# Edge counting of a graph network: the one-hot operands of VectorE read from a table by register address, and the byte split and digit sums moved by some groups

## The chip, the cores and the metric

The kernel runs on one core of one Trainium2 chip. The metric is device time in microseconds (us): the median of the runs before is 2482.77 us, of three runs from 2481.85 to 2486.41. The profile shown here is one execution of 2481.51 us, in which 2480.0 us pass from the first to the last instruction.

## The reference, cut to what matters

3125 nodes of 128 features, 103125 edges (each of 50000 random pairs in both directions and a loop at each node), one type of four per edge. The edges are sorted by `dst`.

```
deg  = maximum(segment_sum(ones, dst), 1);  d = deg ** -0.5
h    = relu(layernorm(x))
feat = h
for i in range(10):                                   # ten hops
    agg  = segment_sum(feat[src] * (d[dst] * d[src])[:, None], dst)
    feat = (0.9 * agg + 0.1 * h) * r[i] + (1 - r[i]) * feat
x    = x + feat
emb  = relu(layernorm(x))
for _ in range(4):                                    # four gated steps
    m   = (emb @ W_msg.T + b_msg).reshape(n, 4, 128)
    emb = gru(segment_sum(m[src, type], dst), emb)
out  = x + emb
```

## The kernel before, in words

Both loops multiply by the adjacency matrix, so the kernel first **counts** the edges into a table `big1` in SBUF (counts per source tile, target tile and node, packed as small digits by type) and then does all gathers as matmuls against it. The change touches the counting alone.

**Counting.** The 103125 edges are 825 chunks of 125. The nodes are 125 groups (`Q`) of 25 targets. For each group q the sorted edges lie in a window of at most 8 chunks (`W`), which begins at chunk `lo`; `windows[q]` holds `lo` and `windows[q + MANY]` the number of chunks over 8, which is zero nearly always. Three tables lie in SBUF with a chunk to a column and an edge of it to a partition: `keys`, and `tab[:, 0]` (the source's place, 0 to 124) and `tab[:, 1]` (the weight). Group q takes these steps:

- GpSimd (POOL), `stage_window` (L384 to L397): waits until the buffer of four groups ago is used (`s_hot_used`), then copies the window of the tables into `win_place`, `win_f` (each entry doubled), `win_w` and `win_key` (doubled, less the group's offset): four small instructions, then `s_wst`.
- VectorE (DVE), `onehots(q, b)` (L1023 to L1057): loads `many` from `windows` into a register; waits for `s_wst` and `s_hot_used`; makes `marks` (8 chunks x 128 places, equal or not; L1038) and `hot_pair` (8 x 228 pairs; L1040); waits for its own `marks`; makes the last three chunks of `weighed` (`marks` times the weight; L1043); branches past the code for further chunks if `many` is zero (L1045). Each entry is doubled so that two neighbouring 16-bit elements are read as a pair.
- ScalarE (ACT), `weigh` (L513 to L517): five activations scale the first five chunks of `marks` into `weighed` by `win_w`.
- TensorE (PE), `count` (L658 to L681): eight matmuls of `weighed` by `hot_pair` add into one of the eight PSUM banks; then `s_hot_used`.
- ScalarE, `evacuate` (L491 to L498): two groups later the bank goes to `words`, a column of its block.

All one-hot buffers are four deep (`DEPTH`), so VectorE can be at most four groups ahead of TensorE.

**Blocks.** Eight groups (`BQ`) are a block; there are 16 (`NB`), the last of five groups. When a block's eight columns are in `words`, ScalarE splits its bytes into `packed` in three instructions, `part_lane` 0, 1, 2 (L500 to L511), of 1800, 1800 and 1400 bytes a partition. They stand in its order at groups 3, 4 and 5 of the next block. Lane 0 waits until `packed` of two blocks ago has been summed and stored. Then VectorE, `sum_digits(blk, b)` (L1059 to L1070), makes the digits in five instructions (L1064 to L1068) and writes them into `big1`. In VectorE's order these stand after group 6 of the next block; the first of them waits for the bytes (`s_bytes`). The SyncE queue stores each `packed` to HBM.

**Order.** Each engine's order is written out by hand. VectorE's counting is eight groups in a row, then a loop of three rounds of four blocks (`Fori`, register-held q), then two blocks in line, the last five groups, `sum_digits(14)`, the mean and variance of `x` (L1125 to L917), and `sum_digits(15)`. Then TensorE sums the degrees from `big1` (L712), and the hops and steps follow.

Of the kernel before, what the change touches and what calls it, by code (L numbers as in the profile page):

```python
# [7 lines left out]
ALU = mybir.AluOpType  # L8
ACT = mybir.ActivationFunctionType
AX = mybir.AxisListType  # L10
ds = bass.ds
# [5 lines left out]
Q = N // TILES  # L17
# [70 lines left out]
def build(nc, x, src, dst, edge_type, layer_reg, w_msg, b_msg, w_ih, w_hh, b_ih, b_hh, out):  # L88
# [7 lines left out]
    with ctx:  # L96
        def sb(name, shape, dt, where=None):
            return (where or ctx).enter_context(nc.sbuf_tensor(name, shape, dt))

        def sem(name):  # L100
            return ctx.enter_context(nc.semaphore(name))
# [63 lines left out]
        with ExitStack() as b:  # L165
            keys = sb("keys", [128, PAD], F32, b)
            tab = sb("tab", [128, 2, PAD], F16, b)
            win = sb("win", [128, 2, 2, W], F32, b)
            win_key = sb("win_key", [128, DEPTH, W, 2], F16, b)
            win_place = sb("win_place", [128, DEPTH, W, 2], F16, b)  # L170
            win_f = sb("win_f", [128, DEPTH, W, 2], F16, b)
            win_w = sb("win_w", [128, DEPTH, W], F32, b)
            win_p = sb("win_p", [128, 2, W], F16, b)
            win_x = sb("win_x", [128, 3], F32, b)
            hot_pair_x = sb("hot_pair_x", [128, KP], F16, b)
            hot_place = sb("hot_place", [128, 2, 128, W], F16, b)
            hot_place_x = sb("hot_place_x", [128, 128], F16, b)
            iota_pair = sb("iota_pair", [128, KP], F16, b)
            iota_row = sb("iota_row", [128, 128], F16, b)
            iota_place = sb("iota_place", [128, 128, W], F16, b)  # L180
            q_off = sb("q_off", [128, QB], F32, b)
            stat_x = sb("stat_x", [128, TILES, 6], F32, b)
# [84 lines left out]
        s_sq, s_sqr = sem("variance_made"), sem("root_made")  # L267
        s_prep = sem("staging_free")
        s_wst, s_pairs, s_hot_used = sem("window_staged"), sem("pair_onehots_made"), sem("onehots_used")
        s_marks, s_weighed = sem("place_onehots_made"), sem("place_onehots_weighed")  # L270
        s_weighed_d = sem("last_places_weighed")
        s_xs_g = sem("extra_weighed")
# [79 lines left out]
        def _(pool):  # L352
# [32 lines left out]
            def stage_window(q, b):  # L385
                lo = pool.value_load(windows[0:1, ds(q, 1)], min_val=0, max_val=NCH)
                pool.wait_ge(s_hot_used, q + 1)

                def twice(m):
                    return m.rearrange("p (w o) -> p w o", o=1).broadcast_to([CH, W, 2])  # L390

                pool.tensor_copy(win_place[0:CH, b, :, :], twice(tab[0:CH, 0, ds(lo, W)]))
                pool.tensor_copy(win_f[0:CH, b, :, :], twice(tab[0:CH, 1, ds(lo, W)]))
                pool.tensor_copy(win_w[0:CH, b, :], tab[0:CH, 1, ds(lo, W)])  # L394
                pool.tensor_tensor(win_key[0:CH, b, :, :], twice(keys[0:CH, ds(lo, W)]),  # L395
                                   q_off[0:CH, ds(q, 1)].rearrange("p (w o) -> p w o", o=1).broadcast_to([CH, W, 2]),
                                   ALU.subtract).then_inc(s_wst, 1)  # L397
# [50 lines left out]
        def _(act):  # L448
# [21 lines left out]
            act.wait_ge(s_prep, 1)  # L470
            act.wait_ge(s_wout, 1)

            act.wait_ge(s_const, 10)
            act.wait_ge(s_win_in, 16)
            act.sem_inc(s_taken, BANKS)
# [24 lines left out]
            def part_lane(turn, b, l, last):  # L500
                blk = 2 * turn + b
                if l == 0:
                    act.wait_ge(s_taken, last + 1 + BANKS)
                    act.wait_ge(s_digits, blk + 1)
                    act.wait_ge(s_packed[b], 16 * turn + 16)
                lanes = words[:, b, :, :].bitcast(U8).rearrange("p n (q l) -> p (n q) l", l=4)
                n = min(LANE, TILES - l * LANE) * TILES * BQ
                at = l * LANE * TILES * BQ
                ins = act.activation(packed[:, b, at:at + n], lanes[:, 0:n, l], ACT.Copy)  # L509
                if l == LANES - 1:  # L510
                    ins.then_inc(s_bytes, 1)  # L511
# [7 lines left out]
            def block_of(turn, b, n, turn_before):  # L519
                blk = 2 * turn + b  # L520
                for j in range(n):
                    weigh(BQ * blk + j, j % DEPTH)
                    if j >= 2:
                        evacuate(blk, b, j - 2)
                    elif turn_before is not None:
                        evacuate(2 * turn_before + 1 - b, 1 - b, BQ - 2 + j)
                    if 3 <= j < 3 + LANES and turn_before is not None:
                        part_lane(turn_before, 1 - b, j - 3, 16 * turn_before + BQ * (1 - b) + BQ - 1)

            block_of(0, 0, BQ, None)  # L530
            with act.Fori(0, (NB - 2) // ROUND) as i:
# [6 lines left out]
                block_of(turn + 1, 0, BQ, turn)  # L538
            block_of(NB // 2 - 1, 1, Q - (NB - 1) * BQ, NB // 2 - 1)
            evacuate(NB - 1, 1, 3)  # L540
            part_lane(NB // 2 - 1, 0, 2, BQ * (NB - 1) - 1)
            evacuate(NB - 1, 1, 4)
            for l in range(LANES):
                part_lane(NB // 2 - 1, 1, l, Q - 1)
# [357 lines left out]
        def _(dve):  # L902
# [120 lines left out]
            def onehots(q, b):  # L1023

                many = dve.value_load(windows[0:1, ds(q + MANY, 1)], min_val=0, max_val=NCH)
                dve.wait_ge(s_wst, q + 1)
                dve.wait_ge(s_hot_used, q + 1)

                def by_two(m, n):
                    return m.rearrange("p w (n two) -> p w n two", two=2)  # L1030

                def row(m, count, n):
                    return m.rearrange("p (o n two) -> p o n two", o=1, two=2).broadcast_to([CH, count, n // 2, 2])

                def each(m, count, n):
                    return m.rearrange("p w (o two) -> p w o two", o=1).broadcast_to([CH, count, n // 2, 2])

                TT(by_two(marks[0:CH, b, :, :], 128), row(iota_row[0:CH, :], W, 128),  # L1038
                   each(win_place[0:CH, b, :, :], W, 128), ALU.is_equal).then_inc(s_marks, 1)
                TT(by_two(hot_pair[0:CH, b, :, :], KP), row(iota_pair[0:CH, :], W, KP),  # L1040
                   each(win_key[0:CH, b, :, :], W, KP), ALU.is_equal).then_inc(s_pairs, 1)
                dve.wait_ge(s_marks, q + 1)
                TT(by_two(weighed[0:CH, b, WA:W, :], 128), by_two(marks[0:CH, b, WA:W, :], 128),  # L1043
                   each(win_f[0:CH, b, WA:W, :], WD, 128), ALU.mult).then_inc(s_weighed_d, 1)
                with dve.If(many > 0):  # L1045
                    lo = dve.value_load(windows[0:1, ds(q, 1)], min_val=0, max_val=NCH - 1)
                    with dve.Fori(0, many) as j:
                        dve.reg_add(made, made, 1)
                        dve.wait_ge(s_more_used, dve.snap(made))
                        col = nc.s_assert_within(lo + j + W, 0, PAD - 1)  # L1050
                        TS(win_x[0:CH, 0:1], keys[0:CH, ds(col, 1)], q_off[0:CH, ds(q, 1)], None, ALU.subtract)
                        dve.tensor_copy(win_x[0:CH, 1:3], tab[0:CH, :, ds(col, 1)].rearrange("p j o -> p (j o)"))\
                           .then_inc(s_xs, 1)
                        dve.wait_ge(s_xs, dve.snap(made))
                        TS(hot_place_x[0:CH, :], iota_place[0:CH, :, 0], win_x[0:CH, 1:2], None, ALU.is_equal)
                        TS(hot_pair_x[0:CH, :], iota_pair[0:CH, :], win_x[0:CH, 0:1], win_x[0:CH, 2:3],
                           ALU.is_equal, ALU.mult).then_inc(s_more, 1)  # L1057
# [41 lines left out]
                        TS(hot_pair_g[0:CH, W, :], iota_pair_g[0:CH, :], win_x[0:CH, 0:1], win_x[0:CH, 2:3],  # L1099
                           ALU.is_equal, ALU.mult).then_inc(s_more_g, 1)  # L1100

            for j in range(BQ):
                onehots(j, j % DEPTH)
            def block_of(blk, b):

                for j in range(BQ):
                    onehots(BQ * (blk + 1) + j, j % DEPTH)
                    if j == BQ - 2:
                        sum_digits(blk, b)

            with dve.Fori(0, (NB - 2) // ROUND) as i:
                steps.loop(i, 4 * ROUND)
                for k in range(ROUND):
                    block_of(ROUND * i + k, k % 2)
            steps.done((NB - 2) // ROUND)
            for blk in range((NB - 2) // ROUND * ROUND, NB - 2):
                block_of(blk, blk % 2)
            for q in range(BQ * (NB - 1), Q):
                onehots(q, q % DEPTH)
            sum_digits(NB - 2, 0)  # L1120
            dve.wait_ge(s_wout, 1)

            dve.wait_ge(s_x, 16)
# [5 lines left out]
            step(last)  # L1129
            TS(to_hd[0:Q, 1, :], stats[0:Q, :, 0], -1.0, None, ALU.mult).then_inc(s_mean, 1)  # L1130
            root_of(stats[0:Q, :, 1], EPS)
            sum_digits(NB - 1, 1)
            one_over_root(rstd[0:Q, :], 1)

# [420 lines left out]
```

## Time and profile before

| | |
|---|---|
| median of three runs | 2482.77 us |
| the profiled execution | 2481.51 us |
| its span, first to last instruction | 2480.0 us |
| TensorE busy | 2164.4 us (87%) |
| VectorE busy | 1392.8 us (56%) |
| ScalarE busy | 502.2 us (20%) |
| GpSimd busy | 236.5 us (10%) |
| before the first group | up to 64.4 us |
| counting, first `marks` to last `marks` | 64.45 to 447.82 us |
| degree sums of TensorE begin | 473.22 us |

Times in the rows are microseconds from the span's start unless marked ns. PE is TensorE, PEld its weight loads, DVE VectorE, ACT ScalarE, POOL GpSimd. A `q` behind an engine's name (DVEq) is its sequencer: loads of registers, arithmetic on them, checks, branches and bare semaphore waits, none of which counts as busy. L1038 is line 1038 of the kernel. A name as `marks<-iota_row,win_place` says what is written and what is read.

### The profile page before, as it was taken

How to read it: one execution, taken by the hardware profiler on the slowest of the kernel's cores; microseconds unless marked ns; L12 is line 12 of the kernel's file. 1: busy time of each engine (PE TensorE's matmuls, PEld its weight loads, DVE VectorE, ACT ScalarE, POOL GpSimd, SP SyncE). 2: the span in 40 equal slices, each digit the busy share in tenths (PEclk: the TensorE clock that was granted, in tenths of full speed). 3: DMA queues.
4: the chain of work that ended last, by engine and by line, in shares of the span. 5: the costliest groups of instructions: out<-in, count | busy, mean ns of one | idle time of the engine just before them, and what ended most of it. 6: DMA issues, size and time to landing. Idle time of an engine off the chain costs nothing.

```text
span 2480.0 us, 40786 instructions
## 1 busy us (share of the span) xinstructions
PE 2164.4 (87%) x14375; PEld 1409.1 (57%) x14886; DVE 1392.8 (56%) x2707; ACT 502.2 (20%) x1119; POOL 236.5 (10%) x517
## 2 busy tenths in 40 slices
PE   1645555499999999999799999999999999999997
PEld 1323222388998989888544465444654446544464
DVE  6878788677777777777732246322464224642243
ACT  0868778510000000000310012100121000210000
POOL 1756556100000000000000000000000000000000
PEclk9656556599999999999899999999999999999998
DMA  2000000000000000003200000000000000000001
GB/s 75 12 32 22 32 21 29 30 24 2 2 2 2 2 2 2 2 2 109 85 1 1 1 1 1 1 1 1 1 1 1 1 1 1 1 1 1 1 1 52
DMA packets 22185, 34.31 MB, mean 14 GB/s; under 512 B 2450, under 2 KB 18442, under 8 KB 21469
## 3 DMA queue, kind: packets, MB, share of 16 engines
q1 hardware_dynamic: 19025, 30.56, 3.6%
q8 instruction: 128, 2.10, 0.4%
q10 hardware_dynamic: 2944, 0.93, 0.2%
q14 instruction: 88, 0.72, 0.1%
HBM read 18.04 MB, written 13.45 MB: 13 GB/s over the span
## 4 chain that ended last, share of the span: by engine, by line
PE 77%; DVE 8%; ACT 6%; issue 4%; DMA 2%; ACTq 1%; DVEq 1%; POOL 1%; POOLq 0%
PE ps L852 42%; PE ps L771 26%; PE ps L804 3%; ACT weighed L516 3%; PE ps L792 2%; ACT packed L509 2%; ACT words L498 1%; ACTq L489 1%; DVE marks L1038 1%; DVE dig L1066 1%; DVE big L1068 1%; DMA big<-in_L_gnn_w_hh 1%; DMA x_after_hops<-x 1%; PE ps L712 1%; PE ps L668 1%
## 5 line engine op out<-in xcount | busy, mean ns | idle before, releaser
L852 PE MATMUL ps<-slots,m_parts 125*128 125x500 fp8e4 (+1 forms) x5600 | 1083.8, 353 | 1.4 <-DVE slots L1338 1.0
L852 PEld LDWEIGHTS ps<-slots,m_parts 125*128 125x128 f16 x5600 | 546.5, 98 | 488.2 <-issue 0.8
L771 PE MATMUL ps<-parts,big 125*128 125x256 f16 x6125 | 669.6, 273 | 6.2 <-DVEq L1385 4.0
L771 PEld LDWEIGHTS ps<-parts,big 125*128 125x128 fp8e4 x6125 | 591.2, 98 | 63.5
L1338 DVE TENSOR_SCALAR slots<-big 128x3200 int32<-128x3200 int32 (+1 forms) x112 | 244.1, 2183 | 280.4 <-PE ps L852 280.4
L668 PE MATMUL ps<-hot_pair,weighed 125*128 125x228 f16 x1000 | 209.9, 358 | 207.6 <-ACT weighed L516 121.7
L668 PEld LDWEIGHTS ps<-hot_pair,weighed 125*128 125x128 f16 x1000 | 113.4, 120 | 303.9 <-ACT weighed L516 266.3
L516 ACT ACTIVATE weighed<-marks,win_w 125x128 f16<-125x128 f16 x625 | 195.5, 389 | 121.0 <-DVE marks L1038 119.9
L1440 DVE SCALAR_TENSOR_TENSOR r_parts<-ps,over,r_parts 128x500 f16<-128x500 f32 (+1 forms) x28 | 19.1, 683 | 230.1 <-ACT r_parts L586 230.1
L1447 DVE SCALAR_TENSOR_TENSOR gate_r<-ps,over,gate_r 128x500 f32<-128x500 f32 (+1 forms) x28 | 19.1, 682 | 228.6 <-PE ps L804 228.6
L462 ACT ACTIVATE rs<-rs 125x25 f32<-125x25 f32 x3 | 0.7, 224 | 716.1 <-DVE rs L917 716.1
L1266 DVE SCALAR_TENSOR_TENSOR hop_tmp<-ps,coef,g 125x128 f32<-125x128 f32 x250 | 87.5, 350 | 102.6 <-PE ps L771 95.3
L586 ACT ACTIVATE r_parts<-ps,over 128x500 f16<-128x500 f32 (+1 forms) x28 | 17.8, 634 | 619.3 <-PE ps L852 619.3
L1040 DVE TENSOR_TENSOR hot_pair<-iota_pair,win_key 125x1824 f16<-125x1824 f16 x125 | 137.5, 1100 | 0.0
L1038 DVE TENSOR_TENSOR marks<-iota_row,win_place 125x1024 f16<-125x1024 f16 x125 | 86.0, 688 | 43.7 <-POOL win_key L395 24.3
L792 PE MATMUL ps<-w_parts,emb_parts 128*125 128x512 f16 x300 | 83.4, 393 | 19.3 <-DVE m_full L1426 10.8
L1268 DVE SCALAR_TENSOR_TENSOR hop_tmp<-ps,coef,hop_tmp 125x128 f32<-125x128 f32 x250 | 87.7, 351 | 8.8
L394 POOL CAST win_w<-tab 125x8 f32 x125 | 85.3, 683 | 0.0
L1261 DVE SCALAR_TENSOR_TENSOR g<-hd,anchor,hop_tmp 125x128 f32<-125x128 f32 x225 | 79.0, 351 | 9.4 <-DVE hop_tmp L1260 0.7
L1247 DVE TENSOR_SCALAR parts<-hop_tmp,scale 125x128 f16<-125x128 f32 x225 | 64.4, 286 | 35.0 <-DVE hop_tmp L1268 31.7
L1250 DVE SCALAR_TENSOR_TENSOR parts<-hop_tmp,scale,parts 125x128 f16<-125x128 f32 x225 | 79.2, 352 | 8.0
L578 ACT ACTIVATE m_parts<-m_full 125x512 f16<-125x512 f32 x100 | 62.6, 630 | 88.6 <-DVE m_full L1426 88.5
(203 smaller groups left out, 1329.8 us busy)
## 6 DMA issues: line engine op xcount, KB each, us to landing
packed_counts<-packed SPq DMA_DIRECT2D x16, 625.0 KB, 2.9
big<-packed_counts SPq DMA_DIRECT2D x4, 1600.0 KB, 7.3
big<-packed_counts SPq DMA_DIRECT2D x3, 1200.0 KB, 6.5
hd<-in_x SPq DMA_DIRECT2D x1, 1562.5 KB
x_again<-in_x SPq DMA_DIRECT2D x1, 1562.5 KB
x_after_hops<-x SPq DMA_DIRECT2D x1, 1562.5 KB
big<-x_after_hops SPq DMA_DIRECT2D x1, 1562.5 KB
out<-big SPq DMA_DIRECT2D x4, 250.0 KB
```

Source lines behind the costliest of these rows:

```text
L394: pool.tensor_copy(win_w[0:CH, b, :], tab[0:CH, 1, ds(lo, W)])
L516: act.activation(weighed[0:CH, b, w, :], marks[0:CH, b, w, :], ACT.Copy, scale=win_w[0:CH, b, w:w + 1]).then_inc(s_weighed, 1)
L668: last = pe.matmul(ps[:, j, 0:KP], weighed[0:CH, b, w, :], hot_pair[0:CH, b, w, :], start=w == 0, stop=w == W - 1, skip_group_check=True)
L771: last = pe.matmul(ps[:, n % RING, 0:2 * F], tot_f8[0:Q, c, a, :], both((parts0, parts1)[par], a), start=a == 0, stop=a == TILES - 1)
L792: last = pe.matmul(ps[0:Q, 6 + a % 2, :], emb_parts[:, h, a, :], w_parts[:, w, :], start=n == 0, stop=n == 2)
L852: last = pe.matmul(ps[:, k % 2, 0:SIZES[k] * Q], m_parts[0:Q, a, h, t * F:(t + 1) * F], slots_f8[0:Q, t % 2, 0:SIZES[k], a, 0:Q], start=a ...
L1038: TT(by_two(marks[0:CH, b, :, :], 128), row(iota_row[0:CH, :], W, 128), each(win_place[0:CH, b, :, :], W, 128), ALU.is_equal).then_inc(s_m ...
L1040: TT(by_two(hot_pair[0:CH, b, :, :], KP), row(iota_pair[0:CH, :], W, KP), each(win_key[0:CH, b, :, :], W, KP), ALU.is_equal).then_inc(s_pa ...
L1250: return STT(out=at[:, 1, :], in0=value, scalar=power, in1=at[:, 0, :], op0=ALU.mult, op1=ALU.subtract)
L1266: step(STT(out=hop_tmp[0:Q, 0, :], in0=bank[:, 0:F], scalar=column(coef, c), in1=tile_of(g, c), op0=ALU.mult, op1=ALU.add))
L1268: step(STT(out=hop_tmp[0:Q, 1, :], in0=bank[:, F:2 * F], scalar=column(coef, c), in1=hop_tmp[0:Q, 0, :], op0=ALU.mult, op1=ALU.add))
L1338: TS(slots[:, t % 2, 0:n * 4].bitcast(I32).rearrange("p (n b w) -> p n b w", b=NB, w=2), big1[:, first:first + n * 4].bitcast(I32).rearran ...
```

## The change

Four things change, all in the counting.

1. GpSimd no longer makes `win_place` and `win_f`. ScalarE, ahead of the counting, copies both rows of `tab` with each entry doubled into a new table `tab_two` (two activations of 1680 elements a partition, after `s_trc`); VectorE waits once for it (`s_two`).
2. `onehots` loads `lo` from `windows` into a register beside `many`, and reads `tab_two[..., ds(lo, W), :]` for `marks` and `tab_two[..., ds(lo + WA, WD), :]` for `weighed`.
3. `part_lane` 0, 1, 2 stand at groups 2, 3 and 4 of the next block.
4. `sum_digits(blk - 2)` stands after group 1 of block `blk`, where `sum_digits(blk)` stood after group 6 of block `blk + 1`. The first two blocks are in line, then three rounds of four blocks, then two blocks in line. `sum_digits(14)` stands behind the mean and variance of `x`, ahead of `sum_digits(15)`.

```diff
-                pool.tensor_copy(win_place[0:CH, b, :, :], twice(tab[0:CH, 0, ds(lo, W)]))
-                pool.tensor_copy(win_f[0:CH, b, :, :], twice(tab[0:CH, 1, ds(lo, W)]))
...
+            act.wait_ge(s_trc, 3)
+            for j in range(2):
+                ins = act.activation(tab_two[0:CH, j, :, :], tab[0:CH, j, :].rearrange("p (k o) -> p k o", o=1)
+                                     .broadcast_to([CH, PAD, 2]), ACT.Copy)
+            ins.then_inc(s_two, 1)
...
-                    if 3 <= j < 3 + LANES and turn_before is not None:
-                        part_lane(turn_before, 1 - b, j - 3, 16 * turn_before + BQ * (1 - b) + BQ - 1)
+                    if 2 <= j < 2 + LANES and turn_before is not None:
+                        part_lane(turn_before, 1 - b, j - 2, 16 * turn_before + BQ * (1 - b) + BQ - 1)
...
             evacuate(NB - 1, 1, 3)
-            part_lane(NB // 2 - 1, 0, 2, BQ * (NB - 1) - 1)
             evacuate(NB - 1, 1, 4)
...
                 many = dve.value_load(windows[0:1, ds(q + MANY, 1)], min_val=0, max_val=NCH)
+                lo = dve.value_load(windows[0:1, ds(q, 1)], min_val=0, max_val=NCH)
+                weights_from = nc.s_assert_within(lo + WA, 0, PAD - WD)
...
-                   each(win_place[0:CH, b, :, :], W, 128), ALU.is_equal).then_inc(s_marks, 1)
+                   each(tab_two[0:CH, 0, ds(lo, W), :], W, 128), ALU.is_equal).then_inc(s_marks, 1)
...
-                   each(win_f[0:CH, b, WA:W, :], WD, 128), ALU.mult).then_inc(s_weighed_d, 1)
+                   each(tab_two[0:CH, 1, ds(weights_from, WD), :], WD, 128), ALU.mult).then_inc(s_weighed_d, 1)
...
-            for j in range(BQ):
+            dve.wait_ge(s_two, 1)
+
+            def block_of(blk, b, n=BQ):
+
+                for j in range(n):
+                    onehots(BQ * blk + j, j % DEPTH)
+                    if j == 1:
+                        sum_digits(blk - 2, b)
+
+            for j in range(2 * BQ):
                 onehots(j, j % DEPTH)
-            def block_of(blk, b):
-
-                for j in range(BQ):
-                    onehots(BQ * (blk + 1) + j, j % DEPTH)
-                    if j == BQ - 2:
-                        sum_digits(blk, b)
-
-            with dve.Fori(0, (NB - 2) // ROUND) as i:
+            TURNS = (NB - 3) // ROUND
+            with dve.Fori(0, TURNS) as i:
                 steps.loop(i, 4 * ROUND)
                 for k in range(ROUND):
-                    block_of(ROUND * i + k, k % 2)
-            steps.done((NB - 2) // ROUND)
-            for blk in range((NB - 2) // ROUND * ROUND, NB - 2):
+                    block_of(ROUND * i + k + 2, k % 2)
+            steps.done(TURNS)
+            for blk in range(TURNS * ROUND + 2, NB - 1):
                 block_of(blk, blk % 2)
-            for q in range(BQ * (NB - 1), Q):
-                onehots(q, q % DEPTH)
-            sum_digits(NB - 2, 0)
+            block_of(NB - 1, 1, Q - BQ * (NB - 1))
             dve.wait_ge(s_wout, 1)
...
             root_of(stats[0:Q, :, 1], EPS)
+            sum_digits(NB - 2, 0)
             sum_digits(NB - 1, 1)
```

## Rows read from the trace of the kernel before

**Rows 1.** Windows, the counting: length, busy us (instructions) by engine, clock, DMA.

```profile
64.40:449.80 385.40, 208.62 (x993) 112.83 (x993) 317.36 (x449) 300.36 (x785) 229.10 (x497) 0.61 0.06 24
```

**Rows 2.** Groups by line, counting: shapes, count | busy us, mean ns | idle before, releasers.

```profile
L516 ACT ACTIVATE weighed<-marks,win_w 125x128 f16<-125x128 f16 x625 | 195.5, 389 | 121.0 <-DVE marks L1038 119.9
...
L1038 DVE TENSOR_TENSOR marks<-iota_row,win_place 125x1024 f16<-125x1024 f16 x125 | 86.0, 688 | 43.7 <-POOL win_key L395 24.3 <-DVE big L1068 9.9 <-issue 4.8
...
L509 ACT ACTIVATE packed<-words 128x1800 uint8<-128x1800 uint8 (+1 forms) x48 | 76.4, 1595 | 0.0
...
L1064 DVE TENSOR_SCALAR dig<-packed 128x1250 int32<-128x1250 int32 x15 | 12.2, 813 | 43.0 <-ACT packed L509 43.0
```

**Rows 3.** Timeline, VectorE, one group of the loop: start us, length us, instruction.

```profile
108.73 0.68 DVE L1038 TENSOR_TENSOR marks<-iota_row,win_place 125x1024 f16<-125x1024 f16 x1
...
110.36 0.35 DVE L1043 TENSOR_TENSOR weighed<-marks,win_f 125x384 f16<-125x384 f16 x1
110.62 0.68 DVE L1038 TENSOR_TENSOR marks<-iota_row,win_place 125x1024 f16<-125x1024 f16 x1
```

**Rows 4.** By line, sequencer in that group: ns min/median/max, first to last start us.

```profile
L1045 DVEq COMPARE_BRANCH  x1: 56/56/56, 109.5 to 109.5; - x1
L1025 DVEq FUSED_REGOPS  x2: 57/124/190, 109.7 to 110.1; - x2
L1026 DVEq ALU_OP  x1: 40/40/40, 110.4 to 110.4; - x1
L1027 DVEq EVENT_SEMAPHORE  x1: 21/21/21, 110.5 to 110.5; - x1
```

**Rows 5.** Timeline, VectorE and GpSimd, one group beside staging.

```profile
75.11 0.69 DVE L1038 TENSOR_TENSOR marks<-iota_row,win_place 125x1024 f16<-125x1024 f16 x1
...
77.11 0.19 POOL L392 COPY win_place<-tab 125x16 f16 x1
77.20 0.69 DVE L1038 TENSOR_TENSOR marks<-iota_row,win_place 125x1024 f16<-125x1024 f16 x1
```

**Rows 6.** Timeline, VectorE, a group with digit sums (in brackets: idle before, releaser).

```profile
93.91 0.69 DVE L1038 TENSOR_TENSOR marks<-iota_row,win_place 125x1024 f16<-125x1024 f16 x1
...
98.44 0.81 DVE L1064 TENSOR_SCALAR dig<-packed 128x1250 int32<-128x1250 int32 x1 [2.56 <-ACT packed L509]
...
102.47 1.46 DVE L1068 TENSOR_SCALAR big<-dig 128x1250 int32 x1
104.95 0.69 DVE L1038 TENSOR_TENSOR marks<-iota_row,win_place 125x1024 f16<-125x1024 f16 x1 [1.02 <-issue]
```

**Rows 7.** By line, sequencer, the one window of over eight chunks.

```profile
L1046 DVEq TENSOR_LOAD <-windows_row x1: 303/303/303, 396.6 to 396.6; - x1
L1047 DVEq MOVE  x1: 36/36/36, 397.2 to 397.2; - x1
L1050 DVEq FUSED_REGOPS  x1: 103/103/103, 397.4 to 397.4; - x1
L1051 DVEq FUSED_REGOPS  x1: 59/59/59, 397.6 to 397.6; - x1
```

**Rows 8.** Timeline and by line, a group outside the loop.

```profile
445.92 0.68 DVE L1038 TENSOR_TENSOR marks<-iota_row,win_place 125x1024 f16<-125x1024 f16 x1
L1027 DVEq EVENT_SEMAPHORE  x1: 21/21/21, 447.5 to 447.5; - x1
```

**Rows 9.** By line, sequencer, 140.9 to 142.2 us, a group of 2.07 us.

```profile
L1045 DVEq COMPARE_BRANCH  x1: 56/56/56, 140.9 to 140.9; - x1
L1025 DVEq FUSED_REGOPS  x2: 57/124/190, 141.4 to 141.8; - x2
```

**Rows 10.** Timeline, the end of the counting.

```profile
447.82 0.68 DVE L1038 TENSOR_TENSOR marks<-iota_row,win_place 125x1024 f16<-125x1024 f16 x1
...
460.82 4.93 DVE L1125 BATCH_NORM_STATS2 stat_x<-hd 125x6 f32<-125x128 f32 x25 [0.21 <-DVE big L1068]
...
473.22 16.92 PE L712 MATMUL ps<-ones,big 125*128 125x1 f16 x625 [20.97 <-DVEq L1070]
```

More of the change, by code:

```diff
@@ L169, in build @@
             win_key = sb("win_key", [128, DEPTH, W, 2], F16, b)
-            win_place = sb("win_place", [128, DEPTH, W, 2], F16, b)
-            win_f = sb("win_f", [128, DEPTH, W, 2], F16, b)
+            tab_two = sb("tab_two", [128, 2, PAD, 2], F16, b)
             win_w = sb("win_w", [128, DEPTH, W], F32, b)
@@ L269, in build @@
         s_wst, s_pairs, s_hot_used = sem("window_staged"), sem("pair_onehots_made"), sem("onehots_used")
+        s_two = sem("tables_doubled")
         s_marks, s_weighed = sem("place_onehots_made"), sem("place_onehots_weighed")
@@ L1043, in onehots @@
                 TT(by_two(weighed[0:CH, b, WA:W, :], 128), by_two(marks[0:CH, b, WA:W, :], 128),
-                   each(win_f[0:CH, b, WA:W, :], WD, 128), ALU.mult).then_inc(s_weighed_d, 1)
+                   each(tab_two[0:CH, 1, ds(weights_from, WD), :], WD, 128), ALU.mult).then_inc(s_weighed_d, 1)
                 with dve.If(many > 0):
-                    lo = dve.value_load(windows[0:1, ds(q, 1)], min_val=0, max_val=NCH - 1)
+                    first = dve.value_load(windows[0:1, ds(q, 1)], min_val=0, max_val=NCH - 1)
                     with dve.Fori(0, many) as j:
@@ L1049, in onehots @@
                         dve.wait_ge(s_more_used, dve.snap(made))
-                        col = nc.s_assert_within(lo + j + W, 0, PAD - 1)
+                        col = nc.s_assert_within(first + j + W, 0, PAD - 1)
                         TS(win_x[0:CH, 0:1], keys[0:CH, ds(col, 1)], q_off[0:CH, ds(q, 1)], None, ALU.subtract)
```

## The prediction, made before the changed kernel ran

> **What bounds the counting now.** The windows view comes first. From 64.4 to 449.8 us VectorE is busy 317 of 385 us, ScalarE 300, TensorE 209 at a clock of 0.61 [rows 1]. Nobody is full, so the bound is in waits. The view by lines names them: ScalarE sat 121 us until VectorE's `marks` came, VectorE sat 43 us ahead of the digit sums until ScalarE's bytes came, and 44 us ahead of `marks` for several reasons [rows 2]. The two hold each other up once a block: VectorE waits for the byte split, then ScalarE waits through the digit sums.
>
> The timeline gives the pace in between. A group where nothing is in the way takes 110.62 - 108.73 = 1.89 us on VectorE, and its three instructions leave no gap [rows 3]. The reader should now look at what the sequencer does in that group [rows 4]. The branch behind `weighed` is at 109.5, 0.74 us after `marks` began, so just when `marks` (0.68 us) is done: the wait for `marks` holds the sequencer, though `weighed` itself runs only at 110.36. Only then comes the value load: register arithmetic at 109.7, the load, arithmetic and a check until 110.4, and the bare wait at 110.5. From the start of that wait to the earliest next `marks` I put 0.08 us, an estimate: its own 0.02 and some 0.05, which the sequencer takes from one step to the next (0.303 us of load [rows 7] and the others leave gaps of this size). From `marks` to the earliest next `marks` the sequencer thus needs 1.73 + 0.08 = 1.81 us. It is hidden behind 1.89 us of VectorE's work with 0.08 us to spare. Beside GpSimd's staging a group takes 2.09 us (75.11 to 77.20), a small copy standing just ahead of `marks` [rows 5].
>
> A group with digit sums takes 104.95 - 93.91 = 11.04 us: 2.56 are the wait for bytes, 5.49 the five sums (98.44 to 103.93), and 1.02 the sequencer's chain behind them, which nothing hides [rows 6]. There are 14 of these, from 10.3 to 11.4 us, 155.8 us in all. The whole stretch of 124 intervals is 447.82 - 64.45 = 383.4 us [rows 10], so the 110 plain ones take 227.6 us, 2.07 us each. In these are two loop ends at 2.95 us extra each, and the one long window at 1.3 us extra, 7.2 us together; without them it is 2.00 us.
>
> **The change, part by part.**
>
> *Split and digit sums moved.* ScalarE's bytes of a block are now ready after group 4 of the next one, and VectorE asks for them after group 1 of the one behind: five groups later. The wait of 2.56 us goes, 14 times: 36 us. ScalarE's lane 0 needs the sums of two blocks before, nine groups old by then, and the store of them, older still: no new wait. What is late next is VectorE itself. ScalarE's work in a block is 8 x 1.81 us (five activations and an evacuation without a wait) + 4.5 us for three lanes (48 x 1.6 us in all [rows 2], less overlaps) = 19 us, less than VectorE's 22 at best, and four buffers carry it over the three groups in which it is slower. The SyncE queue issues the same 16 stores a little earlier.
>
> *Two GpSimd copies fewer.* At most this brings plain groups from 2.00 to 1.89 us, 110 x 0.11 = 12 us. The Trainium skill, SBUF — State Buffer, section "SBUF: two separate sides", says the port pair that VectorE and GpSimd share is an exclusive lock for a whole instruction, the loser fully blocked. By that, 250 copies of 0.19 us could give back 47 us; the trace shows 0.20 us in the groups where they meet [rows 5] and none in others [rows 3], and the sum goes by the 12. Even these are worth nothing once the next part sets the pace.
>
> *A second register load in every group.* This is the large term. Behind the same branch the sequencer now also loads `lo`. The trace has the price of a second load: the one long window does it, from 396.6 until the next step at 397.2, 0.61 us to the hundredth [rows 7]. In the loop, where q is a register, the first load takes from 109.7 to 110.4, 0.72 us with its address [rows 4]. I take 0.72 in the loop and 0.61 outside. `marks` itself now has an address from a register; ahead of such an instruction stand 0.06 us of arithmetic (L1051 [rows 7]) and again some 0.05 to the next step: 0.11. `weighed` has one too, but its arithmetic falls while `marks` runs, where the sequencer waits anyway: nothing, and if that cover is missing, 0.11. The stated bound of `lo + WA` may cost a check: from nothing, as it follows from that of `lo`, to 0.2 us, what one costs beside the long window (397.4 to 397.6 [rows 7]); I take 0.05. At times the sequencer starts later without cause in the kernel: in one group the arithmetic is 0.5 us after the branch, not 0.2 [rows 9], and the group takes 2.07 us. That is about every fifth group; with more instructions, every third or fourth, and now at full price: 0.06 each. These groups are also the proof that the sequencer's chain sets the pace once it passes 1.89 us.
>
> So a plain group in the loop takes 1.81 + 0.72 + 0.11 + 0.05 + 0.06 = 2.75 us. Outside, the wait is at 447.5 with `marks` at 445.92 [rows 8], so 1.53 + 0.08 = 1.61, and with 0.61 + 0.22 it is about 2.45 us. A group with digit sums: 11.04 - 2.56 + 0.88 + 0.05 = 9.4 us in the loop, 9.0 outside.
>
> *The doubled table.* ScalarE is idle from 29 us until the counting, the tables are there at some 39 us, and two copies of 1680 elements are at most 1.7 us each (a lane of 1800 is 1.7): over well before 55 us, when the windows arrive. Nothing. The reads keep their 4-byte pairs, at the price of today.
>
> *Sum.* The loop now holds 96 groups, 84 plain and 12 with sums; outside are 26 plain and 2.
>
> 84 x 2.75 + 26 x 2.45 + 12 x 9.4 + 2 x 9.0 + 7.2 = 231.0 + 63.7 + 112.8 + 18.0 + 7.2 = 432.7 us, against 383.4: +49.3 us.
>
> *The end.* Today the sums of block 14 wait for their bytes behind the last group; mean and variance begin 13.0 us after the last `marks` (460.82 - 447.82), and they and the sums of block 15 take 12.4 us until TensorE's degree sums begin at 473.22, 25.4 us after it [rows 10]. Now they begin at 2.2 us (`weighed` ends at 2.0, as in [rows 3]), and 12.4 + 5.5 for block 14's sums bring the degree sums to 20.1. That is -5.3 us. Behind it nothing changes.
>
> Together +44.0 us, on 2481.5 us of the profiled execution: 2525.5. The median of the runs is 1.3 us above that execution, so about **2526 us**.
>
> Bounds of this case. Low: 0.61 for the load, 0.06 for the address, no check, no late starts: 2.48 and 2.22 us plain, 9.15 and 8.9 with sums, 400.8 us, so +12 us: 2494. High: 0.2 for the check and 0.1 for late starts: 2.94, 2.64, 9.55 and 9.15, 455.7 us, +67 us: 2549. The change breaks even where a plain group in the loop takes 2.37 us, 0.56 above today's chain; the second load alone passes that.
>
> **The rivals.**
>
> *The load hides (faster).* If the sequencer goes on loading while `weighed` waits for `marks`, it has 0.6 us more, and VectorE's instructions set the pace: plain groups 1.92 us, with sums 8.6, so 211 + 120 + 7 = 338.6 us, -44.8 - 5.3 = -50 us: 2432. The Trainium skill, Perfetto Trace Analysis, section "DVE / Act Engine Instruction", has this: an instruction waiting for a semaphore is pushed to a wait queue, and the sequencer is then free for the next. Against it stands the branch at 0.74 us in every group, whatever VectorE did before [rows 4]: what the sequencer executes itself does not pass a waiting instruction. It decides if the added chain behind the branch is under 0.56 us in the loop. Chance 0.10.
>
> *They cancel.* The load costs only part of its price, some 0.35 us, as when the two loads' arithmetic is merged: within 5 us of before, 2482. Nothing in the rows shows loads merged. Chance 0.03.
>
> *The table's reads are slow (slower still).* At a register's address the reads might fall back to one element a cycle. `marks` runs at twice the rate that L1068 has (1250 elements in 1.46 us [rows 6]); halved it takes 0.53 us more, and the branch waits for it: 124 x 0.53 = 66 us on top, 2592. Against it: `weighed` reads pairs from an odd offset already and is not slow for its 384 elements (0.35 us). Chance 0.05.
>
> *The moved sums bring nothing.* If the sums still waited 2.56 us for bytes, 36 us would stay: 2562. Five groups of slack speak against it. Chance 0.02.
>
> **How the numbers follow.** My forecast has a chance of 0.80. A difference of under 0.2% (5 us) can't be told from no change here. Slower: 0.80 less the low tail of 0.01, with 0.07 of the last two: 0.86; same: 0.02 to 0.03; faster: 0.11. The range that holds 8 in 10 is the forecast's own from 2494 to 2549, widened a little at each end, 2490 to 2555; left out are 0.10 below and 0.07 above, and a little more.
>
> **What would show it.** In the changed kernel's trace: two loads in each of VectorE's groups, the second starting about 1.7 us after `marks`; plain groups in the loop at 2.6 to 2.9 us with VectorE idle some 0.8 us before each `marks`, put down to issue; no wait for `packed` ahead of L1064's successor; digit groups at 9.4 us; GpSimd busy well under 229 us; the degree sums 20 us behind the last `marks`. I am wrong if plain groups stay at or under 2.3 us, if the branch comes before `marks` is done, or if `marks` is longer than 0.7 us.

## The result, and the profile after

The changed kernel takes 2543.3 us (median of four runs, 2542.0 to 2546.5) against 2482.3: a ratio of 1.0244, 95% interval 1.0227 to 1.0262. It is 61 us slower. Forecast were 2526 us, a range of 2490 to 2555, and a chance of 0.86 of slower. The profiled execution has a span of 2540.5 us, 60.5 more than before.

The counting now lasts from 63.30 to 512.25 us, 448.95 us where it was 383.4. The windows view of that stretch shows, beside [rows 1], that VectorE (322 us busy) and ScalarE (305) do the work of before and GpSimd less (105, not 229), in 66 us more time. TensorE shows 226 us for the same 993 matmuls, where it had 209, still half of the stretch. An engine that does no more and takes longer waits, or isn't fed.

```profile
63.20:515.00 451.80, 226.07 (x993) 122.18 (x993) 322.32 (x454) 304.58 (x787) 105.00 (x248) 0.78 0.05 21
```

The view by lines says where, as in [rows 2] (busy us, mean ns | idle before, releasers):

```profile
L519 ACT ACTIVATE weighed<-marks,win_w 125x128 f16<-125x128 f16 x625 | 195.1, 390 | 159.4 <-DVE marks L1042 159.2
...
L1042 DVE TENSOR_TENSOR marks<-iota_row,tab_two 125x1024 f16<-125x1024 f16 x125 | 86.6, 693 | 141.6 <-POOL win_key L393 73.2 <-issue 65.5 <-PE ps L670 2.9
...
L1068 DVE TENSOR_SCALAR dig<-packed 128x1250 int32<-128x1250 int32 x14 | 11.5, 822 | 0.0
```

The digit sums wait for nothing (0.0, it was 43.0), as the moves promised. `marks` takes 693 ns, as before (688). But VectorE sits idle for 141.6 us ahead of it, 98 more than before. The timeline has a plain group of the loop at 208.61 - 205.84 = 2.77 us, against the 1.89 of [rows 3]:

```profile
205.84 0.69 DVE L1042 TENSOR_TENSOR marks<-iota_row,tab_two 125x1024 f16<-125x1024 f16 x1 [1.83 <-issue]
206.45 1.10 DVE L1044 TENSOR_TENSOR hot_pair<-iota_pair,win_key 125x1824 f16<-125x1824 f16 x1
207.47 0.35 DVE L1047 TENSOR_TENSOR weighed<-marks,tab_two 125x384 f16<-125x384 f16 x1
208.61 0.69 DVE L1042 TENSOR_TENSOR marks<-iota_row,tab_two 125x1024 f16<-125x1024 f16 x1 [0.79 <-issue]
```

The view by line shows the sequencer's steps in just this group, as in [rows 4] (ns min/median/max, first to last start us). Read by their starts, they are one chain without a hole: `marks` done at 206.5, the address of `weighed`, the branch, the first load with its arithmetic and check, the second, one more step of arithmetic, the wait, the address of `marks`.

```profile
L1047 DVEq FUSED_REGOPS  x1: 86/86/86, 206.6 to 206.6; - x1
L1049 DVEq COMPARE_BRANCH  x1: 56/56/56, 206.7 to 206.7; - x1
L1027 DVEq FUSED_REGOPS  x2: 57/124/190, 206.9 to 207.4; - x2
L1027 DVEq TENSOR_LOAD <-windows_row x1: 304/304/304, 207.0 to 207.0; - x1
L1027 DVEq SEQ_ASSERT  x1: 33/33/33, 207.6 to 207.6; - x1
L1028 DVEq FUSED_REGOPS  x2: 53/122/190, 207.7 to 208.1; - x2
L1028 DVEq TENSOR_LOAD <-windows_row x1: 299/299/299, 207.7 to 207.7; - x1
L1028 DVEq SEQ_ASSERT  x1: 23/23/23, 208.3 to 208.3; - x1
L1030 DVEq ALU_OP  x1: 40/40/40, 208.4 to 208.4; - x1
L1031 DVEq EVENT_SEMAPHORE  x1: 21/21/21, 208.4 to 208.4; - x1
L1042 DVEq FUSED_REGOPS  x1: 57/57/57, 208.5 to 208.5; - x1
```

A trap stands in the view by lines: it puts 73.2 us of the idle time down to GpSimd. Of these, 15.3 us stand ahead of the first group of all; the rest is in the groups behind it. The timeline of one such group shows GpSimd's `win_key` done at 131.31, while `marks` starts at 132.04, after 1.05 us of idle time. But this `marks` is that of q = 23 and that `win_key` is of q = 25; the one that `marks` needs had been done since 125.12. From the second group on, a group's own `win_key` ends at least 2.4 us before its `marks`. The view names the last engine that raised the semaphore, but the time went to the sequencer, whose steps it does not count:

```profile
131.09 0.22 POOL L393 TENSOR_TENSOR win_key<-keys,q_off 125x16 f16 x1
...
132.04 0.69 DVE L1042 TENSOR_TENSOR marks<-iota_row,tab_two 125x1024 f16<-125x1024 f16 x1 [1.05 <-POOL win_key L393]
```

At the end of the counting, mean and variance follow the last group at once and the degree sums of TensorE start 532.05 - 512.25 = 19.8 us after the last `marks` (25.4 before [rows 10]):

```profile
512.25 0.69 DVE L1042 TENSOR_TENSOR marks<-iota_row,tab_two 125x1024 f16<-125x1024 f16 x1 [0.55 <-issue]
...
514.14 4.92 DVE L1130 BATCH_NORM_STATS2 stat_x<-hd 125x6 f32<-125x128 f32 x25
...
532.05 16.97 PE L714 MATMUL ps<-ones,big 125*128 125x1 f16 x625 [14.71 <-DVEq L1074]
```

This table is worked out from the starts of `marks` (L1038 before) in each timeline. "Plain" are groups without digit sums and without a loop turn, with the one long window among them; a loop turn is the group in which VectorE jumps back.

| kernel | median us | counting | mean plain | mean with sums | loop turns |
|---|---|---|---|---|---|
| before | 2482 to 2484 | 383.4 | 2.02 | 11.1 | 4.8, 4.8 |
| changed | 2543.3 | 449.0 | 2.84 | 9.2 | 6.7, 6.7 |
| e1_moves | 2458.5 | 364.4 | 2.11 | 8.4 | 9.5, 9.5 |
| e2_moves_load | 2514.2 | 419.5 | 2.59 | 9.1 | 5.7, 5.7 |
| e3_table | 2548.2 | 449.2 | 2.80 | 9.7 | 5.9, 5.8 |
| e4_ahead | 2460.1 | 367.0 | 2.24 | 7.9 | 7.4, 7.3 |
| e5_moves_ahead | 2451.6 | 356.1 | 2.12 | 7.7 | 9.8, 9.7 |
| e6_marks_only | 2523.0 | 428.3 | 2.67 | 9.2 | 5.8, 5.6 |
| e7_ahead_unchecked | 2436.8 | 344.2 | 2.04 | 7.8 | 7.0, 6.9 |
| e8_ahead_inline | 2426.2 | 330.8 | 2.03 | 7.6 | none |
| e9_moves_inline | 2438.6 | 345.2 | 2.10 | 8.2 | none |

### The profile page after: what moved, and what is told of

It is laid out like the page before. It is cut to its first block, busy times and chain, and to the rows that moved or that the text cites. A ratio compares the mean times of both kernels' runs of the same rounds, so it can differ in the third digit from the quotient of the medians.

```text
span 2540.5 us, 41134 instructions
## 1 busy us (share of the span) xinstructions
PE 2184.1 (86%) x14375; PEld 1419.8 (56%) x14886; DVE 1397.1 (55%) x2707; ACT 507.4 (20%) x1121; POOL 112.5 (4%) x267
## 4 chain that ended last, share of the span: by engine, by line
PE 75%; DVE 11%; DVEq 6%; issue 5%; DMA 2%; ACT 1%; POOLq 0%; ACTq 0%; POOL 0%
PE ps L854 41%; PE ps L773 26%; PE ps L806 3%; DVE marks L1042 3%; DVEq L1028 3%; DVEq L1027 3%; PE ps L794 2%; DVE dig L1070 1%; DVE big L1072 1%; DMA big<-in_L_gnn_w_hh 1%; PE ps L714 1%; DMA x_after_hops<-x 1%; PE ps L758 1%; DVE weighed L1047 1%; DVE hot_pair L1044 1%
## 5 line engine op out<-in xcount | busy, mean ns | idle before, releaser
L670 PE MATMUL ps<-hot_pair,weighed 125*128 125x228 f16 x1000 | 227.7, 388 | 255.5 <-DVE hot_pair L1044 160.7
L670 PEld LDWEIGHTS ps<-hot_pair,weighed 125*128 125x128 f16 x1000 | 122.9, 127 | 359.9 <-ACT weighed L519 307.3
L1042 DVE TENSOR_TENSOR marks<-iota_row,tab_two 125x1024 f16<-125x1024 f16 x125 | 86.6, 693 | 141.6 <-POOL win_key L393 73.2
L392 POOL CAST win_w<-tab 125x8 f32 x125 | 71.7, 574 | 337.8 <-PE ps L670 330.6
```

What stands on the lines that cost most here:

```text
L670: last = pe.matmul(ps[:, j, 0:KP], weighed[0:CH, b, w, :], hot_pair[0:CH, b, w, :], start=w == 0, stop=w == W - 1, skip_group_check=True)
```

## The experiments

The table runs ahead: `e1_moves` and the rest are the experiments below. The theory that they test: VectorE's sequencer, held until `marks` is done and then loading registers, sets the pace of the changed kernel, and the moves by themselves are good. The rivals: the reads at a register's address or the moves are to blame; the parts simply add up; the loads cost the same wherever they stand.

**e1_moves.** The moves alone.

```diff
-                lo = dve.value_load(windows[0:1, ds(q, 1)], min_val=0, max_val=NCH)
-                weights_from = nc.s_assert_within(lo + WA, 0, PAD - WD)
...
-                   each(tab_two[0:CH, 0, ds(lo, W), :], W, 128), ALU.is_equal).then_inc(s_marks, 1)
+                   each(win_place[0:CH, b, :, :], W, 128), ALU.is_equal).then_inc(s_marks, 1)
```

> The changed kernel with the doubled table and the second load undone: GpSimd stages win_place and win_f again, VectorE loads only many; byte split and digit sums stay where the change put them. My theory (VectorE's sequencer chain behind the wait for marks sets the pace of the changed kernel, and the moves by themselves are good): plain groups 1.9 to 2.1 us, digit groups 8.2 to 8.5 us with no wait for the bytes, degree sums 20 us behind the last marks: 383.4 - 14 x 2.6 = 347 us of counting and 5.6 us at the end, so 2440 us (2430 to 2450). Rival (the moves themselves bring ScalarE or the buffers into the way, and are part of the loss): 2482 or more.

Measured: 2458.5 us, ratio 0.9897 (0.9880 to 0.9913). The moves are good, by 25 us and not 43. Digit groups are at 8.4 us, as expected. The missing 18 us are in plain groups of 2.11 us and in two loop turns of 9.5 us. Rather more than half of the plain groups look like the one below: GpSimd's `win_key` ends at 119.56, `marks` starts at 119.60. In 58 of the plain groups `marks` starts within 0.15 us of the end of its own `win_key`; they take 2.24 us in the mean, the others 1.92. So here it is GpSimd that sets the pace of many groups.

```profile
117.51 0.69 DVE L1037 TENSOR_TENSOR marks<-iota_row,win_place 125x1024 f16<-125x1024 f16 x1 [0.53 <-POOL win_key L395]
117.55 0.71 POOL L393 COPY win_f<-tab 125x16 f16 x1
...
118.12 1.10 DVE L1039 TENSOR_TENSOR hot_pair<-iota_pair,win_key 125x1824 f16<-125x1824 f16 x1
118.20 1.07 POOL L394 CAST win_w<-tab 125x8 f32 x1
...
119.23 0.33 POOL L395 TENSOR_TENSOR win_key<-keys,q_off 125x16 f16 x1
119.60 0.69 DVE L1037 TENSOR_TENSOR marks<-iota_row,win_place 125x1024 f16<-125x1024 f16 x1
```

**e2_moves_load.** One line more than e1_moves, and no reader for it.

```diff
                 many = dve.value_load(windows[0:1, ds(q + MANY, 1)], min_val=0, max_val=NCH)
+                lo = dve.value_load(windows[0:1, ds(q, 1)], min_val=0, max_val=NCH)
```

> e1_moves with one thing added: VectorE also loads lo into a register in every group, and nothing reads it. My theory: the load alone makes the sequencer's chain 1.81 + 0.72 = 2.53 us in the loop and 1.61 + 0.61 = 2.22 outside, plus about 0.1 for late starts; digit groups 9.2 and 8.8 us: counting about 420 us, 2513 us (2500 to 2525), so some 73 us over e1_moves. Rival (it is the reads at a register's address, or the port they share, that cost): the same as e1_moves within 5 us.

Measured: 2514.2 us, ratio 1.0127 (1.0110 to 1.0144), 56 us over e1_moves, where 73 were expected; its own time is met to 1 us, e1_moves' was not. A plain group takes 232.64 - 230.14 = 2.50 us (2.53 expected), and VectorE sits 0.53 us ahead of `marks` with all of GpSimd's four instructions back in place:

```profile
230.14 0.69 DVE L1038 TENSOR_TENSOR marks<-iota_row,win_place 125x1024 f16<-125x1024 f16 x1 [0.56 <-issue]
...
232.64 0.69 DVE L1038 TENSOR_TENSOR marks<-iota_row,win_place 125x1024 f16<-125x1024 f16 x1 [0.53 <-POOL win_key L395]
```

(In the second row the view names GpSimd again; this group's own `win_key` had been done since 221.62.) A load that nobody reads turns the gain of the moves into a loss. From here to the changed kernel it is 29 us more: the two addresses, less whatever GpSimd's shorter staging gives.

**e3_table.** The kernel before with the table, the second load and the reads at a register's address, without the moves.

```diff
+                lo = dve.value_load(windows[0:1, ds(q, 1)], min_val=0, max_val=NCH)
+                weights_from = nc.s_assert_within(lo + WA, 0, PAD - WD)
...
-                   each(win_place[0:CH, b, :, :], W, 128), ALU.is_equal).then_inc(s_marks, 1)
+                   each(tab_two[0:CH, 0, ds(lo, W), :], W, 128), ALU.is_equal).then_inc(s_marks, 1)
```

> The kernel before with the doubled table and the second load alone; byte split and digit sums stay where they were. My theory: plain groups 2.88 us in the loop and 2.65 outside as in the changed kernel. With VectorE that much slower, ScalarE has the bytes ready in time, so there is no 2.6 us wait that the moves could take away: digit groups 9.3 to 9.6 us, and only the 5.6 us at the end are missing: 2550 us (2545 to 2560). The moves are thus worth under 10 us here. Rival (the parts add up, the moves are worth some 43 us with either pace): 2586 us.

Measured: 2548.2 us, ratio 1.0259 (1.0242 to 1.0276). So the moves are worth some 5 us beside the loads, of the 25 that they bring alone. These 5 us are all at the end: the counting takes 449 us in both kernels, and the degree sums start 24.8 us behind the last `marks` here, 19.8 in the changed kernel. The sums that waited 2.56 us for their bytes [rows 6] wait 0.22 in the group below (0.22 to 0.85 in all fourteen), in the same order of work, since the slower VectorE comes later:

```profile
104.15 0.81 DVE L1069 TENSOR_SCALAR dig<-packed 128x1250 int32<-128x1250 int32 x1 [0.22 <-ACT packed L512]
```

**e4_ahead.** Every instruction of the changed kernel, the loads for the next group ahead of the wait.

```diff
+                following = window(then) if then is not None else None
                 dve.wait_ge(s_marks, q + 1)
                 TT(by_two(weighed[0:CH, b, WA:W, :], 128), by_two(marks[0:CH, b, WA:W, :], 128),
```

(`window(q)` is the two loads and the stated bound; `onehots` takes its group's registers as an argument and returns those of the next.)

> The changed kernel with every instruction kept but VectorE's two loads for group q + 1 put between hot_pair and weighed of group q, ahead of the wait for marks; only the first group of each loop turn loads its own. My theory: the loads run while the sequencer would wait for marks (0.13 to 0.74 us after marks began) and end at some 1.6 us; behind them stand weighed's address, the branch, a wait and marks' address, so the next marks come at 2.2 to 2.35 us in the loop, 2.0 to 2.1 outside; digit groups 7.8 to 7.9 us, since behind the sums no load is left: 2465 us (2450 to 2480). Rival (the loads take VectorE's or the sequencer's time wherever they stand): 2543 us, within 5.

Measured: 2460.1 us, ratio 0.9908 (0.9891 to 0.9924): 83 us off the changed kernel by order alone. The plain group is at 156.46 - 154.35 = 2.11 us, a little better than expected; the first load starts at 154.5, 0.15 us after `marks`, and the branch, now behind both loads, is at 156.0:

```profile
154.35 0.69 DVE L1047 TENSOR_TENSOR marks<-iota_row,tab_two 125x1024 f16<-125x1024 f16 x1 [0.39 <-DVE big L1079]
...
156.46 0.69 DVE L1047 TENSOR_TENSOR marks<-iota_row,tab_two 125x1024 f16<-125x1024 f16 x1
```

```profile
L1027 DVEq TENSOR_LOAD <-windows_row x1: 307/307/307, 154.5 to 154.5; - x1
L1028 DVEq TENSOR_LOAD <-windows_row x1: 303/303/303, 155.2 to 155.2; - x1
L1055 DVEq COMPARE_BRANCH  x1: 56/56/56, 156.0 to 156.0; - x1
```

**e5_moves_ahead.** The same order for the one load of e1_moves.

```diff
+                following = window(then) if then is not None else None
                 dve.wait_ge(s_marks, q + 1)
```

> e1_moves with VectorE's one load (many) for group q + 1 put ahead of the wait for marks of group q. In e1_moves 78 of 124 groups ended on GpSimd's staging, whose four small instructions stand against VectorE's three. My theory: the sequencer does not set the pace there, so plain groups stay at 2.1 us; only the digit groups lose the load behind the sums, 14 x 0.6 = 8 us, and the late starts are hidden: 2450 us (2443 to 2456). Rival (the sequencer paces these groups too): plain groups 1.9 us, 2428 us.

Measured: 2451.6 us, ratio 0.9868 (0.9851 to 0.9884). Plain groups stay at 2.12 us: they are not the sequencer's. What goes is in the digit groups, 7.7 us for 8.4. (The expectation says that 78 of 124 groups of e1_moves ended on GpSimd's staging. By the times of `win_key` and `marks` it is 58; the view of waits names GpSimd for 33.)

**e6_marks_only.** `weighed` reads a staged `win_f` again, `marks` the table; both loads stay.

```diff
-                   each(tab_two[0:CH, 1, ds(weights_from, WD), :], WD, 128), ALU.mult).then_inc(s_weighed_d, 1)
+                   each(win_f[0:CH, b, WA:W, :], WD, 128), ALU.mult).then_inc(s_weighed_d, 1)
```

> The changed kernel with one of the two reads at a register's address undone: weighed reads win_f, which GpSimd stages again (three instructions a group), marks still reads the table, both loads stay. The prediction held the address arithmetic of weighed to be hidden; in the changed kernel's trace the branch stands at 0.89 us after marks, not 0.74. My theory: that arithmetic stands in the chain with its full 0.15 us: 124 x 0.15 = 18 us less, 2525 us (2520 to 2530), with the branch back at 0.74. Rival (it is hidden, and the branch is late for another reason, such as the longer code): 2543 us.

Measured: 2523.0 us, ratio 1.0157 (1.0140 to 1.0174), 20 us under the changed kernel. A plain group takes 203.03 - 200.42 = 2.61 us, 0.16 less, and the branch is back at 0.74 us after `marks` (201.2):

```profile
200.42 0.69 DVE L1043 TENSOR_TENSOR marks<-iota_row,tab_two 125x1024 f16<-125x1024 f16 x1 [1.83 <-issue]
...
203.03 0.69 DVE L1043 TENSOR_TENSOR marks<-iota_row,tab_two 125x1024 f16<-125x1024 f16 x1 [0.63 <-issue]
```

```profile
L1050 DVEq COMPARE_BRANCH  x1: 56/56/56, 201.2 to 201.2; - x1
```

**e7_ahead_unchecked.** e4_ahead without the check of `many`.

```diff
-                many = dve.value_load(windows[0:1, ds(q + MANY, 1)], min_val=0, max_val=NCH)
+                many = dve.value_load(windows[0:1, ds(q + MANY, 1)])
```

> e4_ahead with many loaded without its bounds, so without 0.19 us of arithmetic and the 0.02 us check behind the load (a checked load stays beside the long window). In e4_ahead the sequencer still set the pace at 2.11 us a plain group in the loop. My theory: the chain falls by 0.22 us to 1.89 us, just VectorE's own work: plain groups 1.9 to 1.95 us, 107 x 0.2 = 21 us less than e4_ahead, 2438 us (2430 to 2445). Rival (2.11 us is GpSimd's or the buffers' doing): 2460 us.

Measured: 2436.8 us, ratio 0.9811 (0.9795 to 0.9827), 23 us under e4_ahead. Two groups in a row take 1.89 and 1.90 us, VectorE's own work with no idle time in front; the mean of 2.04 holds late starts, the long window and some waits that the view puts down to GpSimd (16 groups behind the first).

```profile
155.97 0.68 DVE L1047 TENSOR_TENSOR marks<-iota_row,tab_two 125x1024 f16<-125x1024 f16 x1
...
157.86 0.69 DVE L1047 TENSOR_TENSOR marks<-iota_row,tab_two 125x1024 f16<-125x1024 f16 x1
...
159.76 0.69 DVE L1047 TENSOR_TENSOR marks<-iota_row,tab_two 125x1024 f16<-125x1024 f16 x1
```

It is 15 us under e5_moves_ahead, which has no table. That is what the table is worth once the loads are hidden, as GpSimd stages two instructions a group, not four (the two kernels also differ in the check of `many`, which was not tried apart).

**e8_ahead_inline.** e7_ahead_unchecked with VectorE's counting in line.

```diff
-            with dve.Fori(0, TURNS) as i:
-                steps.loop(i, 4 * ROUND)
...
+            for blk in range(2, NB - 1):
                 found = block_of(blk, blk % 2, found)
```

> e7_ahead_unchecked with all of VectorE's counting in line instead of three turns of a loop. My theory: the two jumps back cost 7.4 us each in e4_ahead against 2.1 for a plain group, so 10 to 11 us go with them; the load of q's address arithmetic goes too but is hidden by now: 2427 us (2420 to 2433). Rival (code that runs straight through is fetched no faster than code that jumps back, so that late starts grow with its length): as e7_ahead_unchecked or slower.

Measured: 2426.2 us, ratio 0.9764 (0.9748 to 0.9780), 10.6 under e7_ahead_unchecked. This is the best version: 57 us under the kernel before, 117 under the changed one. In e7_ahead_unchecked the turn that goes looked like this:

```profile
183.50 0.37 DVE L1053 TENSOR_TENSOR weighed<-marks,tab_two 125x384 f16<-125x384 f16 x1
188.86 0.69 DVE L1047 TENSOR_TENSOR marks<-iota_row,tab_two 125x1024 f16<-125x1024 f16 x1 [5.00 <-POOL win_key L393]
```

**e9_moves_inline.** e1_moves in line, for the 18 us that it had missed.

```diff
-            with dve.Fori(0, TURNS) as i:
...
+            for blk in range(2, NB - 1):
                 block_of(blk, blk % 2)
```

> e1_moves came 18 us above its expectation. Its trace has two groups of 9.45 and 9.48 us where VectorE's loop turns (4.84 us in the kernel before), and plain groups of 2.11 us, not 2.0. This is e1_moves with VectorE's counting in line. If the jumps back are the first part of the miss, 2 x 7.4 = 15 us go and nothing else moves, as GpSimd paces the plain groups: 2444 us (2438 to 2448). Rival (the wait at the loop's turn belongs to the staging or the buffers, and comes back elsewhere): 2458 us.

Measured: 2438.6 us (five runs, 2435.3 to 2443.5), ratio 0.9822 (0.9806 to 0.9838). 20 us go: 15 with the two turns, and 0.2 to 0.3 us in nearly each digit group, where the arithmetic on q no longer stands in the sequencer's chain behind the sums. So the turns were the larger part of the miss; plain groups stay GpSimd's at 2.10 us.

## Why the prediction was right, and where it was off

*The second load is the large term.* Right, in mechanism and price: e2_moves_load shows 2.50 us a group for 2.53, e4_ahead takes it back by order alone. The row that told it was the one that left the sequencer 0.08 us to spare.

*The rival "the load hides" fell.* In every group of the changed kernel the branch stands no sooner than 0.88 us after `marks`, and in every group of the kernel before and of e6_marks_only, where no arithmetic stands between, at 0.72 to 0.79. What the Trainium skill states (Perfetto Trace Analysis, section "DVE / Act Engine Instruction"), that the sequencer is free once an instruction that waits is pushed, does not hold here for the steps that it executes itself: none of them passed the waiting `weighed`. e4_ahead shows the same from the other side: put ahead of that wait, the loads run during `marks`. And it is the wait that holds them, not a full queue in front of VectorE: in a digit group of e1_moves the arithmetic that stands behind the first two sums (L76) is done at 224.9, when `weighed` (225.48) and both sums (225.75 and 226.47) have yet to start, none of them with a wait still open.

*The moves take away 14 x 2.56 us.* Right for the digit groups (8.4 us alone, 9.2 with the loads, 9.4 forecast). But most of this was not the moves': e3_table has 9.7 us without them. The sum took the wait away and then slowed VectorE, and so could not show that the slowing alone would have taken most of it; the result is the same, the credit is not.

*The table's reads keep their rate.* Right: `marks` 693 ns, `weighed` 352.

*The step that failed: "`weighed` has one too, but its arithmetic falls while `marks` runs, where the sequencer waits anyway: nothing".* It stands behind the wait, at 0.73 us, and costs 0.15 us in every group: e6_marks_only gives 20 us back without it. The price named for a missing cover was 0.11. The check of `lo + WA`, put at 0.05, is not there at all. A group without a late start is at 2.77 in the loop where 2.69 was forecast.

*Late starts.* 0.06 us a group was mis-sized: without the long window the means are 2.88 in the loop and 2.65 outside, 0.11 and 0.12 over the groups without one. Against the forecast 2.75 and 2.45, the 81 and 26 plain groups have 10.3 + 5.2 = 15.5 us more, mainly from these two terms. The loop turns and the long window added 2.7, the digit groups gave back 2.0: +16.3 in the counting (not rounded, 16.25), and with -1.2 at the start (the first `marks` is at 62.8 to 64.5 us among these kernels, without a pattern), -0.3 at the end and 1.7 behind the degree sums, which I did not trace, the 16.5 us between +44.0 and +60.5. (The prediction's last step has a slip besides: 2525.5 + 1.3 is 2526.8, not 2526.)

*GpSimd's copies.* That they were worth at most 12 us, and nothing behind the loads, fits the changed kernel, where no group but the first starts on the end of its own staging; no run takes them apart there. The rule of the exclusive port pair (the Trainium skill, SBUF — State Buffer, section "SBUF: two separate sides") put 47 us on them. Where the sequencer no longer sets the pace, e7_ahead_unchecked against e5_moves_ahead has 15 us, nearer the rows' bound. The rows of e1_moves show which side is held there: beside `marks` and `hot_pair` GpSimd's copies take 0.71 and 1.07 us, where an unhindered one takes 0.19 [rows 5], and each ends 0.05 us after VectorE's instruction does, while `marks` keeps its 0.69. So GpSimd does pace many groups of e1_moves and e5_moves_ahead, but by its chain of four held instructions between VectorE's three.

## What to carry to other kernels

Before adding a register load to an inner loop, read the sequencer's steps by line and add up its chain from the wait that holds it to the next instruction: here 1.81 us stood behind 1.89 us of work, and 0.72 us of load had no room. Put the loads ahead of the wait on the engine's own result, not behind it; the same should hold for address arithmetic, which no run moved. And price a removed wait in the schedule that remains: here a slower VectorE had already removed it, and a gain of 25 us alone was 5 us together.

## What the runs showed that I had not expected

- The turn of VectorE's loop has no fixed price: 4.8 us before, 9.5 in e1_moves, 7.4 in e4_ahead, for a body of 32 groups. In e1_moves 4.9 us pass between the jump and the next step of the sequencer. What sets this time wasn't tried. With the counting in line it is gone, and the kernels are 20 and 11 us faster.
- About every third group of the changed kernel starts 0.2 to 0.4 us late in the loop, and up to 0.7 outside, somewhere in the sequencer's chain, some within a load (752 and 917 ns where 305 is usual). It is not chance: in the loop the same groups are late in each turn (the fifth of the body takes 3.15, 3.14 and 3.13 us), so the lateness goes with the place in the code. Why was not tried. It costs nothing while the chain has slack: in e5_moves_ahead 44 of the 45 plain groups that neither GpSimd, the loop's start and turns nor the long window held take 1.89 to 1.91 us.
- The bounds of a register load cost 0.22 us (arithmetic and check) of its 0.72.
